# Four conditioned transformer blocks on one core: another order of the opening, q stacks filled by ScalarE, and the residuals' rows loaded behind the maxima

## What is computed

```python
def block(x, cond, l):            # layers 0, 1, 3; layer 1 is causal
    shift1, scale1, gate1, shift2, scale2, gate2 = split(silu_or_id(cond) @ W_ada + b_ada, 6)
    h = layernorm(x) * (1 + scale1) + shift1
    q, k, v = (h @ Wq + bq), (h @ Wk + bk), (h @ Wv + bv)        # 16 heads of 16
    o = softmax(q @ k.T / 4) @ v                                  # per head, 256 x 256 scores
    x = x + gate1 * (o @ Wo + bo)
    h = layernorm(x) * (1 + scale2) + shift2
    return x + gate2 * (gelu(h @ W1 + b1) @ W2 + b2)              # 1024 hidden

def block2(x, cond):              # layer 2 has no MLP
    h1 = x + out_proj(softmax(q @ k.T) / 16 @ v)                  # q, k, v of modulated layernorm(x)
    return modulated_layernorm(h1) + h1
```

## Time and profile before

| | us |
|---|---|
| median of 3 runs | 1216.07 |
| lowest, highest | 1214.62, 1216.55 |
| the profiled execution | 1208.6 |
| its span | 1206.8 |

### The profile page before, as it was taken

The page is one execution under the profiler, slowest core; times in us unless marked ns, Lnnn a source line. Parts: engine busy times, 40 slices in busy tenths (PEclk is TensorE's granted clock), DMA queues, the critical chain, the costliest instruction groups (busy, mean ns, idle before and its releaser), DMA issues.

```text
span 1206.8 us, 22214 instructions
## 1 busy us (share of the span) xinstructions
PE 1107.2 (92%) x7540; PEld 843.7 (70%) x7540; DVE 814.8 (68%) x2245; ACT 554.2 (46%) x1120; POOL 180.1 (15%) x290
## 2 busy tenths in 40 slices
PE   6799999999999999999999888888888999999996
PEld 4567777777777777777777665555555777777765
DVE  5566677666677667766667677777778656776642
ACT  1235655555543455444455334444444446555451
POOL 5011111101102211011111001111114101011010
PEclk9679999999999999999999999999999999999998
DMA  7713332123343333312333413333343233322300
GB/s 264 212 48 106 107 106 75 62 76 105 107 150 131 93 107 106 94 58 66 103 107 116 130 57 113 113 110 113 106 154 119 64 99 116 116 72 67 92 25 18
DMA packets 102714, 123.18 MB, mean 102 GB/s; under 512 B 8992, under 2 KB 96032, under 8 KB 101600
## 3 DMA queue, kind: packets, MB, share of 16 engines
q1 hardware_dynamic: 102048, 121.73, 32.5%
q10 hardware_dynamic: 576, 0.30, 0.1%
HBM read 85.16 MB, written 35.78 MB: 100 GB/s over the span
## 4 chain that ended last, share of the span: by engine, by line
PE 70%; DVE 14%; issue 5%; DMA 5%; ACT 4%; ACTq 1%; SPq 0%; POOL 0%; DVEq 0%; POOLq 0%
PE dense L1162 12%; PE dense L1148 10%; PE dense L1093 9%; PE s_bank L1186 9%; PE o_bank L1241 8%; PE st_bank L1223 7%; DMA q_stack<-max_t 5%; DVE neg_max L793 4%; PE o_bank L1122 3%; PE o_bank L1108 2%; PE o_bank L1072 2%; PE s_bank L1196 2%; PE o_bank L1248 2%; ACT xn L553 2%; DVE s_bank L788 1%
## 5 line engine op out<-in xcount | busy, mean ns | idle before, releaser
L605 ACT ACTIVATE probs<-st_bank 128x512 f32<-128x512 f32 (+1 forms) x512 | 263.9, 568 | 263.3 <-PE st_bank L1223 202.7
L793 DVE TENSOR_REDUCE neg_max<-s_bank 128x2 f32<-128x512 f32 x384 | 256.3, 684 | 65.8 <-PE s_bank L1186 61.7
L1186 PE MATMUL s_bank<-k_stack,q_stack 96*128 96x256 f32 (+1 forms) x1024 | 231.7, 317 | 9.4 <-DVE neg_max L793 1.7
L1186 PEld LDWEIGHTS s_bank<-k_stack,q_stack 96*128 96x128 f32 x1024 | 165.3, 193 | 60.8 <-issue 24.1
L1162 PE MATMUL dense<-w_sb,hid 128*128 128x256 f32 x768 | 201.0, 380 | 0.0
L1223 PE MATMUL st_bank<-q_stack,k_stack 98*128 98x512 f32 x384 | 153.3, 471 | 13.2 <-DMA q_stack<-max_t 12.3
L443 POOL TENSOR_TENSOR veps<-mv,eps_c 128x2 f32<-128x2 f32 x65 | 12.7, 196 | 990.2 <-DVE mv L759 976.0
L1241 PE MATMUL o_bank<-probs,v_aug 128*32 128x256 f32 (+1 forms) x2048 | 133.4, 379 | 22.2 <-ACT v_aug L545 18.2
L1162 PEld LDWEIGHTS dense<-w_sb,hid 128*128 128x128 f32 x768 | 130.5, 189 | 10.7 <-issue 0.4
L1093 PE MATMUL dense<-ht,w_sb 128*128 128x256 f32 x512 | 128.3, 391 | 4.3 <-DVE row_out L745 3.2
L593 ACT ACTIVATE hid<-dense,vec 128x256 f32<-128x256 f32 x192 | 80.6, 471 | 100.9 <-PE dense L1148 100.8
...
## 6 DMA issues: line engine op xcount, KB each, us to landing
...
```

Source lines behind the costliest of these rows:

```text
L605: nc.scalar.activation(probs[p % 4][:, kt, :, q0:N], src, ACT.Exp, scale=SCORE_SCALE[l]).then_inc(p_sb, 1)
L793: nc.vector.tensor_reduce(neg_max[:, qt, 2 * p:2 * p + 2], split3(bank[:]), AX.X, ALU.max, negate=True).then_inc(s_max, 1)
L1186: ins = mm(bank[:, e * N:e * N + k1], q_stack[g.par][0:KB, 2 * p + e, qt * P:(qt + 1) * P].bitcast(F32R), k_stack[g.par][0:KB, p, 0:k1].bi ...
```

## The change

There are two changes. In the opening, SP's loads come in another order and the later ones move behind `stack` of sequence 0; the fills of `k_stack` and `v_aug` stand elsewhere in DVE's order, both `q_stack`s are filled by ScalarE with an activation of scale 0, and the inputs of sequence 1 (products, high and low parts, spill and stack) are made in step 0. In every plain step SP waits for both halves' maxima of `g` before it issues the load of `par_sb`. In step 0 the loads of the next modulation and of the second MLP matrix stand ahead of that wait.

```diff
 def inputs_of(a):
-    return a.exists and (a.reg is not None or a.off > 1)
+    return a.exists and (a.reg is not None or a.off > 0)
 # SP, start
+    sp.dma_start(vec[:], vecs).then_inc(vec_ld, 16)
     sp.dma_start(ada_sb[:, :, 0:2 * D], ada[0][:, :, 0:2 * D]).then_inc(ada_first_ld, 16)
-    sp.dma_start(vec[:], vecs).then_inc(vec_ld, 16)
+    load_weights(0, 0, O_O, wqkv_ld)
+    sp.dma_start(x_sb[:, 1], ...).then_inc(x_ld[1], 16)
     sp.dma_start(ada_sb[:, :, 2 * D:ADA], ada[0][:, :, 2 * D:ADA]).then_inc(ada_ld, 16)
-    sp.dma_start(x_sb[:, 1], ...).then_inc(x_ld[1], 16)
-    load_weights(0, 0, O_O, wqkv_ld)
     sp.dma_start(row_in[:], rows[0].partition_broadcast(B)).then_inc(row_ld, 16)
     load_weights(0, O_O, O_2, w_ld)
-    load_weights(0, O_2, WCOLS, w2_ld)
-    for t in range(T):
-        sp.dma_start(x_sb[:, 2:B, t], ...).then_inc(x_ld[2], 16)
 # SP, step(g)
     if inputs_of(a):
         spill(a)
+        if a.reg is None and a.off == 1:
+            sp.wait_ge(q_filled, 2)
+            sp.wait_ge(kv_filled, 3)
         stack(a)
+    if g.reg is None and g.off == 0:
+        next_modulation(1)
+        load_weights(0, O_2, WCOLS, w2_ld)
+    if not mlp:
+        wait(sp, max_ld, g.count(64, 64))
 # SP, ahead of the steps
     spill(Step(0))
-    sp.wait_ge(q_filled, 2)
-    sp.wait_ge(kv_filled, 4)
+    sp.wait_ge(q_filled, 1)
+    sp.wait_ge(kv_filled, 1)
     stack(Step(0))
+    for t in range(T):
+        sp.dma_start(x_sb[:, 2:B, t], ...).then_inc(x_ld[2], 16)
     store_rows(0)
-    spill(Step(1))
-    sp.wait_ge(stack_ld, 144)
-    stack(Step(1))
-    sp.wait_ge(max_ld, 32)
-    next_modulation(1)
 # POOL: split_w1(0) moves into step 0, ahead of the wait for par_ld
-    pool.wait_ge(ht1_sb, 1)
-    pick(Step(1), 0, mod1_now)
-    fill_stack(0)
-    fill_stack(1)
-    split_w1(0)
 # ACT
+    def fill_stack(i):
+        nc.scalar.activation(q_stack[i][:].bitcast(F32R), eps_c[:, 0:1]...to_broadcast([P, H, N]), ACT.Copy,
+                             scale=0.0).then_inc(q_filled, 1)
     act.wait_ge(consts, 1)
+    fill_stack(0)
...
-    for first in (Step(0), Step(1)):
-        modulate1(first); query_hi(first); key_hi(first); value_copy(first)
+    modulate1(first); query_hi(first); key_hi(first); value_copy(first)      # first = Step(0)
+    fill_stack(1)
 # DVE
-    fill_stack(0)                      # at the very start
     first_norm(Step(0))
+    memset(k_stack[0])
     modulation_cols(0, (0,))
-    fill_stack(1)
-    modulation_cols(0, (1,))
+    memset(v_aug[0])
     first_norm(Step(1))
+    memset(k_stack[1]); memset(v_aug[1])
     query_lo(Step(0))
     key_lo(Step(0))
+    modulation_cols(0, (1,))
     modulation_rows(0)
-    query_lo(Step(1))
-    key_lo(Step(1))
     maxima(Step(0), *range(8))
 # PE
+    modulation_cols(0, (0,))
     ht1_t(first)
-    modulation_cols(0, (0,))
+    products(first)
     modulation_cols(0, (1,))
-    products(first)
+    ht1_t(Step(1))
     pe.wait_ge(q_lo_sb, 1)
     modulation_rows(0)
-    ht1_t(Step(1))
-    pe.wait_ge(mod_done, 1)
-    products(Step(1))
     score(first, *range(8))
```

31 lines of the change are left out of this document (17 added, 14 removed).

## The result

The changed kernel takes 1202.37 us (median of 4 runs, 1197.58 to 1204.61), beside 1215.34 for the kernel before in the same comparison (4 runs, 1214.58 to 1216.55): a ratio of 0.9887, interval 0.9856 to 0.9919. It is 13 us faster. The forecast was 6.7 us faster, so the gain is nearly twice what was said; 1202.37 lies at the low end of the range of 1202 to 1215.

What follows compares the result with a forecast made beforehand. PE's work and waits were taken to bound the kernel (70% of the chain). Opening -5.3 and step 0 +2.6 give -2.7; with plain steps -4.0 the sum is -6.7 us, median 1216.07 to 1209.4, range 1202 to 1215.

Steps and rivals of the forecast that it cites:

- the two mechanisms: Opening: POOL's fills beside DVE's normalization delay the low parts. Plain steps: the residuals' rows' load delays the maxima.
- the term of +2.6 us for pair 4 in step 0: Step 0: pair 4's exponentials come 2.6 us later after the first ones than before; bounds -0.9 and +6.3.
- 12.8 + 2.4 + 0.6: Step 0, pair 4's exponentials at 15.8: maxima's landing 12.8, delay by the modulation load 2.4, landing to exponentials 0.6.
- the opening: Up to the first exponentials: they start at 47.1 instead of 52.42, 5.3 us earlier, bounds 4 and 8.5.
- the plain steps: Steps 17 to 24: 60% of some 6.6 us of PE's waits for maxima comes back, 4.0 us, bounds 2 and 6.6.
- rival A: Step 0: maxima's packets go ahead of the modulation load, -0.9 instead of +2.6; products may be fast; -12, 1204; chance 0.15.
- The sign named for it: Step 0, PE's wait for the maxima: 3 us or more shows the forecast, none A, 6 B (both large loads first).
- From pair 4 to step 1 nothing changes: Step 0: the stretch from pair 4's exponentials to step 1's first ones stays at 22.12 us.
- just fit: Step 0: residuals' rows land some 4 to 5 us behind the maxima; they are needed 5 us behind pair 4.
- The rule of round robin by packets: Step 0: by packet turns, the small maxima transfer waits one turn of the modulation load, not the MLP matrix too.
- Rival C: Plain steps: k_stack's loads set the maxima's landing, PE gains nothing, POOL waits for late rows; slower, 1223; chance 0.07.
- the 60% that was forecast: Plain steps: share of removed waits that shortens the step, from steps 20 and 21: 0.68 of 1.14.

Runs made afterwards that it cites:

- e5_act_fills: The kernel before with only the two q_stack fills moved from POOL to ScalarE; 1212.12 us, ratio 0.9969 to the kernel before.
- e9_pool_fills: The changed kernel with both q_stack fills on POOL again, the new order kept; 1208.67 us, ratio 0.9939 to the kernel before.
- e7_ada_late: e6_mlp_rows with step 0's modulation load and second MLP matrix issued behind the residuals' rows; 1196.99 us, ratio 0.9857 to the kernel before.
- e8_warm: e6_mlp_rows with 28 unread matmuls in PE's wait ahead of the first scores; 1199.11 us, ratio 0.9868 to the kernel before.
- e0_before: The kernel before, unchanged, with a second profile of its own; 1212.51 us, ratio 0.9988 to the kernel before.
- e6_mlp_rows: The changed kernel with MLP steps' residuals' rows also issued behind the maxima, POOL's power no longer waiting for them; 1195.74 us, ratio 0.9814 to the kernel before.
- e11_double: The kernel before with a second, unread 512 KB load behind the residuals' rows in every step; 1249.16 us, ratio 1.0294 to the kernel before.
- e2_rows: The kernel before with only SP's new wait for the maxima in plain steps; 1205.32 us, ratio 0.9914 to the kernel before.
- e3_busy_before: The kernel before with four unread matmuls ahead of pair 4's transposed scores in steps 17 to 24; 1215.84 us, ratio 0.9989 to the kernel before.

## Why the prediction was right and where it was wrong

In short: the two mechanisms were the ones named, and the forecast gain was little more than half of what came. The step that failed is the term of +2.6 us for pair 4 in step 0, "12.8 + 2.4 + 0.6": it measured -0.3, and the whole of step 0 grew by 0.7 to 0.9 us instead of 2.6. Smaller parts are the opening (1.3 us more than said) and the plain steps, where the sum had no term for the falls of the clock.

**The opening up to the first exponentials: right, in each link.** Products at 12.72 (12.7 said), first stack load at 20.97 (21.8), scores at 31.16 (31.9), from there 15.18 us to the exponentials (15.2), which came at 46.34 (47.1). ScalarE's fills cost 3.60 us each (3 to 4.8) and are hidden. The gain to that point is 6.1 us in the pair of profiles (5.3 said), 6.6 from mean to mean. `e5_act_fills` and `e9_pool_fills` show that the mechanism was the one named: POOL's fills beside DVE's normalization, and this normalization ahead of the low parts. The start of the scores hangs on the first stack load, and that on the low parts.

**Step 0: wrong by 2 us.** Forecast +2.6; it took 36.13 us instead of 35.27 in the pair of profiles (+0.9), 35.99 instead of 35.24 from mean to mean (+0.7). The step that failed is "12.8 + 2.4 + 0.6" for pair 4's exponentials, 15.8 us into the step; they came at 12.82, against 13.15 before. The 12.8 is a landing beside the residuals' rows, which the change itself moves out of the way; without them and without the modulation load the maxima land 3.5 us after their issue (`e7_ada_late`), not 4.91. On that base a collision as in `e8_warm` adds 2.5, as forecast, but in five of eight profiles it adds under 0.5. What I took as a fixed price varies, and its likeliest value lay near rival A's. The sign named for it says the same: a wait of PE of 3 us or more was the forecast, none was A; it was 2.35 and 1.56. But A's 1204, the nearest rival to the result, is so in part by luck: it counted on fast products, and they took 5.26 us.

"From pair 4 to step 1 nothing changes" did not hold in the pair of profiles: that stretch took 23.31 and not 22.12, at a clock of 0.75 instead of 0.84. `e0_before` has 23.41 without any change, so it is not shown that the change did it. Nor did the residuals' rows "just fit": POOL's `power` waited for them until 66.65, 8.4 us behind PE's go-on for pair 4 (58.27), where 5 was said. That did not lengthen the step, since the stretch is no shorter in `e6_mlp_rows`, where `power` does not wait for them (24.53). Together, opening and step 0 gained 5.2 us in the pair of profiles, 5.9 from mean to mean, against 2.7.

**The rule of round robin by packets.** The Trainium skill ("DMA: Bandwidth & Descriptors", section Queues, rings and completion order) has each DMA engine drain a whole packet of one ring before it turns to the next. The runs agree with it so far: were transfers served in the order of their issue alone, a load issued behind the maxima would cost them nothing, and it did cost in step 20 of `e0_before` (0.6 us behind, 4.91 us to go on) and in step 0 (up to 2.5 us). A second load behind the first added nothing in the plain steps of `e11_double`. No run shows the turns themselves.

**The plain steps: mechanism right, size too small.** The waits went from 7.0 to 0.4 us, the eight steps from 241.4 to 238.0 in the pair of profiles, -3.3 where -4.0 was said. Rival C is refuted: the maxima land in time once the rows' load is held back, and in these steps POOL never waits for it. The mean of the profiles says -5.8, the broader mean above -5.0, and the timing of `e2_rows` -10.5, at least -6. Two things are in this. In the steps where the clock stays up in both profiles of the pair (18, 20, 21, 23 and 24), 4.1 us of waits gave back 2.4, close to the 60% that was forecast. Beside that come falls of the clock, for which the sum had no term: among steps 18 to 24 there are eight in six profiles that keep the waits (the five above and `e11_double`), each in a step where PE waited 1.0 us or more, and three in the nine profiles with the new wait; each costs 1.0 us or more. That the waits bring the falls fits this, but is not shown: other steps with waits of 1.0 to 1.3 us have no fall, and the changed kernel has one without a wait. The sum was made from the execution at hand and then set against the median of all: "the profiled execution's 1208.6 would be 1201.9; it lies 7.5 under the median". That carries the whole difference over to the changed kernel as if it were a constant. It is not: the changed kernel's profiles took 1202.65 and 1198.0, beside medians of 1202.37 and 1200.21. A typical execution of before has more to lose than the one shown, by what the medians and the profiles say.

**The balance.** Of the 6.3 us by which the gain was larger than forecast, 3.2 lie in opening and step 0 and 1.0 to 1.8 in the plain steps (means of profiles). The rest would have to lie in the 4 us by which the timed median of before stands above the mean of its three profiled executions. Where these are could not be settled. Over the 72 timed executions the time falls with the mean granted clock (8 us for each 0.01, correlation -0.86), and in the profiles the clock falls in the opening, in step 0, in the plain steps and in the last step, in no other MLP step but those of `e11_double`. But `e3_busy_before` raised the clock by 0.004 and gained nothing, so whether the clock makes the time or the waits make both stays open.
